# A decoder layer on one core: self attention and cross attention run together in rounds of one pair of row tiles

## The reference

```python
# self attention, one head of 256 columns, sigmoid in place of softmax
q, k, v = x @ Wq.T + bq, x @ Wk.T + bk, x @ Wv.T + bv
attn = sigmoid(layer_norm(q) @ layer_norm(k).T / 16 - log(S))     # 1024 x 1024 per sequence
x = layer_norm(x + ((attn @ v) @ Wo.T + bo) * layerscale)
# cross attention, 16 heads of 16 columns, 77 context rows per sequence, softmax
x = layer_norm(x + softmax(qh @ kh.T / 4) @ vh @ dense_w.T + dense_b)
# feed-forward with time mixing
xr, xk = mu_r * x + (1 - mu_r) * x_prev, mu_k * x + (1 - mu_k) * x_prev
x = layer_norm(x + sigmoid(xr @ W_r.T) * (relu(xk @ W_k.T) ** 2 @ W_v.T))
```

## Time and profile before

| what | value |
| --- | --- |
| median of 3 runs | 588.88 us (587.7 to 589.36) |
| the profiled execution | 589.6 us, span 587.6 us from first to last instruction |
| PE busy | 547.7 us, 93% of the span |
| VectorE (DVE) busy | 434.8 us, 74% |
| ScalarE (ACT) busy | 384.0 us, 65% |
| GpSimd (POOL) busy | 340.5 us, 58% |
| ScalarE's table loads | 4 in all, 1.28 us each |
| DMA | 17.53 MB, mean 30 GB/s |
| granted clock of TensorE | 0.982 of full over the span |

### The profile page before, as it was taken

One profiled execution on the slowest core, in us unless ns is written; L12 is line 12 of the kernel. 1 busy time (PEld: TensorE's weight loads), 2 busy tenths in 40 slices (PEclk: granted clock), 3 DMA queues, 4 the chain that ended last, 5 costly groups with the idle time before them and its releaser, 6 DMA issues.

```text
span 587.6 us, 11185 instructions
## 1 busy us (share of the span) xinstructions
PE 547.7 (93%) x3962; PEld 456.4 (78%) x3962; DVE 434.8 (74%) x1017; ACT 384.0 (65%) x1026; POOL 340.5 (58%) x394
## 2 busy tenths in 40 slices
PE   6999999999999999999978999999999976899993
PEld 4788989898989988987865677677667555899993
DVE  4665567766666687657447889899888878699995
ACT  2664343444443444542469889999999885999974
POOL 2655252352534343332329878898888982169996
PEclk9999999999999999999989999999999998999997
DMA  7221001010121002110000000000000000001113
GB/s 171 67 90 54 20 1 54 20 55 18 55 69 40 1 1 73 36 54 1 1 0 2 2 1 2 1 2 1 2 2 1 2 1 1 1 20 56 55 56 107
DMA packets 18383, 17.53 MB, mean 30 GB/s; under 512 B 1867, under 2 KB 18328, under 8 KB 18328
## 3 DMA queue, kind: packets, MB, share of 16 engines
q1 hardware_dynamic: 17624, 16.17, 9.0%
q10 hardware_dynamic: 704, 0.66, 0.4%
HBM read 12.63 MB, written 4.19 MB: 29 GB/s over the span
## 4 chain that ended last, share of the span: by engine, by line
PE 49%; POOL 20%; DVE 14%; ACT 8%; issue 6%; DMA 2%; SPq 0%; POOLq 0%; DVEq 0%; ACTq 0%
PE ring L222 21%; PE big L222 19%; POOL p_sb L697 9%; POOL fold L692 6%; DVE big L1008 3%; ACT p_sb L417 2%; PE ring L1253 2%; POOL xs L684 2%; PE big L1347 2%; DMA xraw<-in_xT 1%; POOL rs L708 1%; DVE xmT_lo L824 1%; PE ring L1363 1%; DVE y L1034 1%; DVE kkT_lo L824 1%
## 5 line engine op out<-in xcount | busy, mean ns | idle before, releaser
L824 DVE TENSOR_TENSOR aT_lo<-a_sb,aT_hi 128x512 fp32r<-128x512 f32 x64 | 45.8, 717 | 78.1 <-ACT aT_hi L331 78.1
L417 ACT ACTIVATE p_sb<-big,neg_mx 128x77 f32<-128x77 f32 x384 | 89.7, 358 | 13.5 <-DVE neg_mx L944 13.4
L697 POOL TENSOR_TENSOR p_sb<-p_sb,rc 128x1248 f32<-128x1248 f32 x32 | 72.8, 2276 | 23.3 <-DVE rc L957 23.3
L222 PE MATMUL big<-vv_hi,aT_hi 128*128 128x256 f32 x256 | 72.7, 284 | 4.0 <-DVE xs L890 4.0
L374 ACT ACTIVATE a_sb<-ring,nlogs 128x512 f32<-128x512 f32 x64 | 43.5, 679 | 50.0 <-PE ring L222 49.9
L222 PE MATMUL big<-vv_hi,aT_lo 128*128 128x256 f32 x256 | 72.4, 283 | 0.0
L222 PE MATMUL big<-vv_lo,aT_hi 128*128 128x256 f32 x256 | 72.4, 283 | 0.0
L1363 PE MATMUL ring<-ident,p_sb 128*128 128x128 f32 (+1 forms) x384 | 55.5, 280 | 8.5 <-DVE pT L964 8.0
L1363 PEld LDWEIGHTS ring<-ident,p_sb 128*128 128x128 f32 (+1 forms) x384 | 40.2, 130 | 29.4 <-issue 20.4
L1347 PE MATMUL big<-kb,xq 64*128 64x308 f32 x192 | 51.2, 483 | 5.8 <-ACT p_sb L417 4.4
L222 PEld LDWEIGHTS big<-vv_hi,aT_hi 128*128 128x128 f32 x256 | 48.8, 191 | 9.1 <-issue 6.8
(11 more groups left out here) (179 smaller groups left out, 1757.2 us busy)
## 6 DMA issues: line engine op xcount, KB each, us to landing
xraw<-in_xT SPq DMA_DIRECT2D x16, 256.0 KB, 2.8
xs<-in_x SPq DMA_DIRECT2D x8, 512.0 KB, 3.9
out_y<-y SPq DMA_DIRECT2D x16, 256.0 KB, 2.1
cT<-in_cT SPq DMA_DIRECT2D x1, 308.0 KB
wraw<-in_wqT ACTq DMA_DIRECT2D x2, 128.0 KB, 3.4
wraw<-in_wkT SPq DMA_DIRECT2D x2, 128.0 KB, 3.5
wv_raw<-in_wv SPq DMA_DIRECT2D x1, 256.0 KB, 5.4
wo_ls<-in_woT ACTq DMA_DIRECT2D x1, 256.0 KB, 5.8
```

The costliest lines, as they stand in the source:

```text
L222: mm = pe.matmul(out, s_, m_, start=first and k == 0 and q == 0, stop=last and k == n - 1 and q == 2, skip_group_check=not check)
L417: ex = act.activation(weights(t)[:, HG * g + h, 0:SC], logits[g][:, h * SC:(h + 1) * SC], ACT.Exp, bias=neg_mx[:, t % 2, HG * g + h:HG * g ...
L697: pool.tensor_tensor(weights(t), weights(t), rc[:, t % 2].rearrange("p (h o) -> p h o", o=1) .to_broadcast([P, H, SP]), ALU.mult).then_inc ...
L824: return dve.tensor_tensor(lo, whole, f(hi), ALU.subtract)
```

## The change

- The work is ordered in 21 rounds (`NR_ALL`), with one function `round_(r)` for each engine. Round `r` holds four self attention steps, which now cover one pair of query tiles (256 rows) by a pair of key tiles, and cross attention work two to five pairs behind: `x1(r-2)`, `query(r-2)`, `cross_scores(2r-5)` and `(2r-4)`, `weights_t(2r-7)` and `(2r-6)`, `mixed(r-4)`, `dense(r-4)`.
- Each of the two attentions has four PSUM banks. Self: `acc` (one bank), `st_bank` (two), `proj` (one, shared by `qk`, `tqk` and `v`). Cross: four banks that hold the logits of a tile, then its transposes (banks 0 and 1), the mixed values (bank 2) and the transposed rows and queries (bank 3). So `cross_scores(t)` waits for the exponentials of tile `t-1` and for the copies of the transposes of tile `t-2`.
- `scores(i)` is 12 matmuls of 256 columns in place of 6 of 512. `attend(i)` is 12 matmuls of 256 columns, as before.
- `cross_scores(t)` is 8 matmuls that contract 32 rows, over 154 columns (2 heads each), in place of 4 that contract 64 rows over 308.
- The weights have 80 columns a head in place of 78, so 1280 columns: 10 transposes of 128 rows a tile in place of 12, and full rows throughout.
- The zero-padded value matrix is put together by 24 small DMAs on the sync queue (`value_pieces`) in place of six matmuls and eight masked copies.
- Sigmoids and exponentials alternate on ScalarE in every round. The dummy exponential goes; `first_sigmoid` stays.
- `qk_norm` on VectorE is `scalar_tensor_tensor` with the negated mean times the deviation, which GpSimd makes with two more small operations a tile. `norm1` moves from VectorE to ScalarE.
- Keys, values of the context and their weights are loaded and made ahead of round 0, in place of near the end of the self attention.
- Only 6 pairs of rows stay on the chip (`NR`). The first ten pairs go to DRAM after `norm2` and come back ahead of the feed-forward.
- The feed-forward begins on every engine after the last round.

```diff
-        big = ctx.enter_context(nc.psum_tensor("big", [P, 3 * BANK], F32))
-        ring = ctx.enter_context(nc.psum_tensor("ring", [P, 5, BANK], F32))
+        acc_ps = ctx.enter_context(nc.psum_tensor("acc", [P, BANK], F32))
+        st_ps = ctx.enter_context(nc.psum_tensor("st", [P, 2, BANK], F32))
+        proj = ctx.enter_context(nc.psum_tensor("proj", [P, BANK], F32))
+        xb = ctx.enter_context(nc.psum_tensor("xb", [P, 4, BANK], F32))
...
             @block.scalar
+                def round_(r):
+                    at(sigmoid, 4 * r - 1, NS)
+                    at(sigmoid_hi, 4 * r - 1, NS)
+                    at(xt_hi, r + 5, NJ, JB + 1)
+                    at(query, r - 2)
+                    at(sigmoid, 4 * r, NS)
+                    at(exponentials, 2 * r - 4, NT)
+                    at(tqk_hi, 2 * r + 7, NT, TB - 1)
+                    at(sigmoid, 4 * r + 1, NS)
+                    at(weights_tail, 2 * r - 5, NT)
+                    at(sigmoid_hi, 4 * r, NS)
+                    at(sigmoid_hi, 4 * r + 1, NS)
+                    at(norm2, r - 5)
+                    at(sigmoid, 4 * r + 2, NS)
+                    at(mixed_hi, r - 3)
+                    at(norm1, r - 1)
+                    at(exponentials, 2 * r - 3, NT)
+                    at(v_hi, r + 4, NJ, JB)
+                    at(tqk_hi, 2 * r + 8, NT, TB - 1)
+                    at(sigmoid_hi, 4 * r + 2, NS)
+                    at(weights_tail, 2 * r - 4, NT)
+                    at(x1_hi, r - 1)
...
             @block.tensor
-                def cross_scores(t, e):
+                def cross_scores(t):
...
                     if t:
-                        w.wait_ge(*ex_act.at(4 * (t - 1) + 2 * e + 1))
+                        w.wait_ge(*ex_act.at(t - 1))
...
+                    if t >= 2:
+                        for c in range(3):
+                            w.wait_ge(*turned(t - 2, c))
+                        if u:
+                            w.wait_ge(*pv_dve.at(i - 1))
+                        elif i >= 2:
+                            w.wait_ge(*xda_dve.at(i - 2))
+                    for e in range(KC):
+                        for n in range(4):
+                            own = slice(32 * n, 32 * (n + 1))
+                            mm = pe.matmul(logits[n][:, e * KW:(e + 1) * KW], xq[own, e * D + u * P:e * D + (u + 1) * P],
+                                           kb[own, b, e], start=True, stop=True)
                     mm.then_inc(xs_pe.sem, 1)
...
                 def weights_t(t, c):
                     w.wait_ge(*pn_pool.at(t))
+                    if c == 2:
+                        w.wait_ge(*turned(t, 0))
+                    elif t + 1 < NT:
+                        w.wait_ge(*ex_act.at(t + 1, c + 1))
...
+                def round_(r):
+                    at(tqk, 2 * r + 5, NT, TB - 1)
+                    at(weights_t, 2 * r - 7, NT, 0, 0)
+                    at(weights_t, 2 * r - 7, NT, 0, 1)
+                    at(scores, 4 * r - 3, NS)
+                    at(weights_t, 2 * r - 7, NT, 0, 2)
+                    at(scores, 4 * r - 2, NS)
+                    at(mixed, r - 4)
+                    at(qk, 2 * r + 6, NT, TB)
+                    at(scores, 4 * r - 1, NS)
+                    at(cross_scores, 2 * r - 5, NT)
+                    at(v, r + 3, NJ, JB)
+                    at(weights_t, 2 * r - 6, NT, 0, 0)
+                    at(scores, 4 * r, NS)
+                    at(weights_t, 2 * r - 6, NT, 0, 1)
+                    at(tqk, 2 * r + 6, NT, TB - 1)
+                    at(dense, r - 4)
+                    at(weights_t, 2 * r - 6, NT, 0, 2)
+                    at(x1, r - 2)
+                    at(attend, 4 * r - 4, NS)
+                    at(qk, 2 * r + 7, NT, TB)
+                    at(query, r - 2)
+                    at(attend, 4 * r - 3, NS)
+                    at(cross_scores, 2 * r - 4, NT)
+                    at(attend, 4 * r - 2, NS)
+                    at(attend, 4 * r - 1, NS)
```

More of the change, by code:

```diff
@@ L70, in wait_ge, with value_pieces @@
             self.eng.wait_ge(sem, value)
+def value_pieces():
+    for n in range(4):
+        for a in range(2):
+            row = SP * (2 * n + a) - P * n
+            first = min(max(P - row, 0), SC)
+            if first:
+                yield n, a, 0, row, 0, first
+            if first < SC:
+                yield n, a, 1, max(row - P, 0), first, SC - first
 def decoder_layer(nc, io):
@@ new lines, in decoder_layer @@
+            kb = tensor(ph, "kb", [P, B, KC, KW])
+            with ExitStack() as own:
+                xT_first = halves(own, "xT_first", [P, NX, KC, 2 * P])
+            vb = tensor(ph, "vb", [P, B, KC, 4, 2, 2 * DH])
+            x1T = halves(ph, "x1T", [P, BANK])
+            xq = tensor(ph, "xq", [P, BANK])
+            mask_k = tensor(ph, "mask_k", [P, KH])
+            neg_mx, sm, rc = (tensor(ph, name, [P, 2, H]) for name in ("neg_mx", "sm", "rc"))
+            fold = tensor(ph, "fold", [P, H * FO])
@@ new lines, in _ @@
+                load_xt(4)
+                load_xt(5)
+                sp.dma_start(wx_raw[:, XQW], rows("xwqT")).then_inc(load2.sem, 16)
+                sp.dma_start(wx_raw[:, XDW], rows("xwdT")).then_inc(load2.sem, 16)
+                load_rows(1)
+                load_xt(6)
+                w.wait_ge(*vb_pool.at(0))
+                w.wait_ge(*vx_dve.at(1))
+                for n, a, half, row, key, count in value_pieces():
+                    for k in range(KC):
+                        sp.dma_start(vb[row:row + count, :, k, n, half, DH * a:DH * (a + 1)],
+                                     v32[key:key + count, :, k, DH * (2 * n + a):DH * (2 * n + a + 1)]).then_inc(vb_dma.sem, 16)
@@ L315, in _ @@
+                w.wait_ge(*av_pe.at(LAST))
+                for n in range(NSP // 2):
+                    load_again(n)
                 for i in range(NJ):
@@ L516, in _ @@
                 tqk_hi(1)
-                for t in range(2, 5):
+                for t in range(2, 6):
                     if t + 1 < NF:
@@ L1279, in attend @@
+                    for kt in range(2):
+                        for t in range(2):
+                            cut = slice(kt * D + t * P, kt * D + (t + 1) * P)
+                            mm = split_product(pe, acc[:, t], [hi_lo(aT, i % NA, cut)], [hi_lo(vv, b % 2, 2 * u + kt)],
+                                               first=u == 0 and kt == 0 and t == 0, last=u == 3 and kt == 1, check=False)
                     mm.then_inc(av_pe.sem, 1)
@@ L1371, in mixed @@
+                    for c in range(3):
+                        w.wait_ge(*turned(2 * i + 1, c))
+                    w.wait_ge(*vb_dma.at(VB_DMA - 1))
+                    if i + 1 < NJ:
+                        w.wait_ge(*ex_act.at(2 * i + 2, 3))
+                    else:
                         w.wait_ge(*xda_dve.at(i - 1))
-                    else:
-                        w.wait_ge(*st_act.at(NS - 1, 1))
                     for k in range(KC):
-                        for first in (True, False):
+                        for half in range(2):
@@ L1528, in _ @@
-                dense(NJ - 3)
-                for c in range(3):
-                    weights_t(NT - 3, c)
+                    tqk(t - 2)
+                    v(t - 4)
+                tqk(6)
+                keys(0)
+                keys(1)
+                values(0)
+                values(1)
+                for r in range(NR_ALL):
+                    round_(r)
                 x2(0)
                 x2(1)
-                mixed(NJ - 2)
-                for c in range(3):
-                    weights_t(NT - 2, c)
@@ L1536, in _ @@
-                dense(NJ - 2)
-                for c in range(3):
-                    weights_t(NT - 1, c)
                 x2(2)
@@ L1545, in _ @@
                 x2(3)
-                dense(NJ - 1)
                 mix_values(0)
```

1038 lines of the change are left out of this document (422 added, 616 removed).

## The result

The changed kernel takes 615.4 us (median of 4 runs, 613.87 to 616.14) beside 588.7 us for the kernel before on the same chip: a ratio of 1.0452, 95% interval 1.0427 to 1.0477. The forecast was 579, the range 562 to 604, and slower had a chance of 0.32.

The account below looks back on a forecast made before the run. PE was taken as the bound in both attention stages. Start 45.5, rounds 391, tail 45 and feed-forward 96 gave a span of 577.5 us, plus 1.3 for 579; range 562 to 604.

Parts of the forecast that it names:

- the waits in a full round: Rounds 4 to 12: nothing waits on paper; 0.7 us of stall put on each, bounds 0 and 2.5, 6.3 us together.
- DVE or the zero-slack places cost more: Rival: stalls of 1.5 to 2 us a round, total 590 to 597 us; chance 0.10.
- the 391 of the sum: All rounds from the first scores to the last self attention step, stalls included: 391 us.
- the tail: Last two cross pairs alone after the last self step, their chain not overlapping: 45 us, with 21 us of PE work.
- The rival with a tail of 55: The change does what it says but the tail eats it: tail 55, start 50, total 593 us; chance 0.05.
- the first four start faster: Feed-forward: first four pairs, with only `carried` and the mixes on ACT, take 12.4 us of the stage's 96.
- The row groups overlap four deep: `cross_scores`: four row groups run at once on PE, so a tile costs 0.72 us for 1.44.
- the rival of 602: Row groups do not overlap four deep: 579 + 23 = 602 us, or about 590 with three quarters won; chance 0.07.
- The table switches: ACT: four table loads a round, about 60 in all, some 80 us beside PE's work; ACT busy 23.6 of 26.15 us.
- The likeliest slower rival: Table switches set the round: 2.2 us a round for 13 rounds, total 599 us; chance 0.17.
- The sign that the prediction set for it: `mixed` 28 us or more apart, with PE waiting for ACT's sigmoid, tail copy or exponentials, would point to the tables.
- The late rounds: Rounds 13 to 16: projections no longer cover the exponentials behind `cross_scores(2r-5)`; a stall of 1.5 us a round, 6 together.

Follow-up runs that it names:

- The one added wait: Changed kernel with POOL starting `xt_lo` and `residual1` only after `qk_norm` is done; 594.8 us, ratio 1.0100 to the kernel before.
- With filler: Changed kernel plus 123 matmuls whose result nobody reads, in gaps of the last three rounds; 606.5 us, ratio 1.0298 to the kernel before.
- the run that has no loads: Changed kernel with Sigmoid in place of Exp in the softmax, so ACT changes no table in the rounds; 612.7 us, ratio 1.0421 to the kernel before.
- all of these mended as far as was tried: Changed kernel with POOL's wait, early scores in rounds 13 to 16, early feed-forward pairs, 42 unread matmuls in round 17; 582.4 us, ratio 0.9932 to the kernel before.
- edits that are alone: Changed kernel with `qk_norm` as `tensor_scalar`, 611.6 us, or with Sigmoid in place of Exp, 612.7 us; both at once, 604.3 us.

## Why the prediction was wrong

**The step that failed** is the one on the waits in a full round: "Nothing waits on paper, but four places have under 0.3 us of slack. I put 0.7 us of stall on each of the rounds 4 to 12". It followed the exponentials, the sigmoids and the copies with their durations from the trace, but took DVE's and POOL's work as sums a round and never laid the one's stream beside the other's. The change's `qk_norm` was costed only by its two small operations on POOL. What the runs show: it stands beside two operations of POOL, the first of which starts 0.08 us earlier, takes 2.89 us for 0.88, and PE waits 1.64 us. A full round is 28.07 us for 26.21 without the collision: a stall of 1.9, over twice the 0.7, but inside the bounds of 0 to 2.5. One round ahead of the fourth, where the sum had no stall, waits as well. The rival "DVE or the zero-slack places cost more" had the size, 1.5 to 2 us a round, at 590 to 597, a chance of 0.10 and no mechanism. The one added wait, which takes this stall away and nothing else, shows it: the first scores to the last attend step take 390.6 us then, for the 391 of the sum. That the total agrees is in part luck: a full round is 26.21 where the sum had 26.85, 5.8 us less over nine, and the first and last rounds take that much more.

The Trainium skill, "SBUF — State Buffer", section "SBUF: two separate sides", says that DVE and GpSimd share a pair of ports under an exclusive lock; a DVE operation in a 2-port mode, or one with two inputs in SBUF against a GpSimd operation that reads SBUF, keeps the other engine out for its whole length if it comes first, and is kept out if it comes second. The trace agrees for operations of 512 columns: 1.0 us more for each one of POOL in the way. It doesn't for POOL's small ones: `qk_norm` of the kernel before took its 0.41 us though up to 0.77 us of an operation of two columns was still to run. The same page, "Summary: rules for kernel authors", has the two scheduled by which of them is off the critical path; to let POOL wait is the edit that brought 20.6 us. The prediction didn't weigh it.

**The second error is a size**: the tail, 45 us in the sum and 56.6 measured. The chain is the one that was written down, but its times came from rows at the 2.4 GHz level, and PE ran it at a granted 0.69, 0.61 in its last 30 us: `mixed` takes 3.64 for 1.93. With filler the tail is 48.3 us (456.3 to 504.6), so 8.3 of the 11.6 are the clock in this execution, and 3 the chain. The rival with a tail of 55 had nearly this size, with a chance of 0.05. The feed-forward starts with a 7.8 us wait for the first mixed rows, where the sum had "the first four start faster", and is 4.1 us longer.

The first lay inside its stated bounds, the second 1.6 us past its rival's. The range had them as cases of their own, and not both in one sum: 579 + 21 + 12 + 4 is 616.

**What was right.** *The row groups overlap four deep*: sixteen passes in 0.74 us (453.67 to 454.41), 0.72 forecast, and the rival of 602 falls. *PE's work*: 26.21 us a round without waits, 26.15 forecast. *The table switches*: 58 loads in the rounds, ACT busy 465 (near 460), all hidden: they begin while ACT waits for its data. The likeliest slower rival, with a chance of 0.17 and 599, falls with the run that has no loads. The sign that the prediction set for it came half true: `mixed` stands 28.07 apart, but what PE waits for in the full rounds is DVE. *Start*: 45.66 for 45.5. *The late rounds*: PE waits 1.7 us for the exponentials, 1.5 forecast. It does so seven times from round 13 on, three of them in the tail. No DMA ends a wait of PE in the profile's list, so the DRAM round trip and the small DMAs are hidden. *PE busy near 525* was 537.6; from 460 to 540 matmuls count longer at the lower clock.

So where did the 26 us of saved work on PE go? The sum itself had given 16 of them back, to a start that puts the first scores at 45.7 for 33.2 and to a tail that the kernel before filled with feed-forward work. The other ten, and 27 more, went to a collision of DVE and POOL (21), to the clock and the chain of the tail (12) and to the start of the feed-forward (4). With all of these mended as far as was tried, the change is worth 0.7%.

**Left open.** Executions of one kernel here lie up to 10 us apart (589.7 to 599.4 with the wait on POOL), more than of the kernel before (585.9 to 589.6 in 20), and medians of edits that are alone don't add up with those that are together (11.1 for 3.8 and 2.7). The traces show where such differences lie, at places that no edit touched: the first scores start between 43.9 and 49.0, a late round takes 22.8 or 24.3, and the tail without filler 53.3 to 56.6, the longer ones at the lower granted clock. So a gain of 3 or 4 us in medians of four executions says little by itself, and what sets the clock differently from one execution to the next is open. That a lock on ports is what holds DVE up is the page's word; the runs show the hold-up and what takes it away. The narrow row groups were not tried alone in the kernel before.

## What to carry to other kernels

When two stages are laid over each other, look in the trace before for instructions of one shape whose durations differ, and read for each tight place what DVE and POOL do at the same moment, not only each engine's own sum: an operation of the engine that has time, started a tenth of a microsecond too early, can hold the path up for its whole length, and a wait added to it is then a gain. Cost a tail in which PE stands half the time at the lower level of its clock, and fill it with work of the next stage. Where errors have places of their own, put them into one range together.

## What the runs showed of the hardware

Both forms of a 256-column float32 normalisation on DVE stood still beside POOL's additions and subtractions of 512 columns: `scalar_tensor_tensor` with two inputs in SBUF, 2.89 us a pair for 0.88, and `tensor_scalar` with one, 2.63 us for 0.73. POOL's own operations, each of which had started first, were hardly longer for it (1.29 and 1.44 us beside 1.28 and 1.30).

Two kinds of neighbours were seen beside each other without a hold-up. A POOL operation of two columns did nothing to `tensor_scalar` in the kernel before (404 to 411 ns in all 52). And a long POOL operation did nothing to a DVE instruction with one input and its output in PSUM: the feed-forward's `scalar_tensor_tensor`, the other input in SBUF, took 0.48 to 0.49 us in all 64, though POOL was in the midst of an operation of over 1.2 us as 45 of them began:

```profile
L1042 DVE SCALAR_TENSOR_TENSOR st<-acc,mu,carry x32: 480/482/493, 515.9 to 588.5; 128x256 f32<-128x256 f32 x32
```

A table load takes 1.28 us, and the activation behind it started 0.01 us after its end (219.54); where an activation waits for data its load runs within that wait, so that 58 of them in 400 us could not be told in the time.
